# Normalised input turned in 32x32 blocks and carried by transfers; order of weighted inputs, first state and first loads changed

## The reference

```
proj = xn @ in_proj                       # gate z (1024), xBC (1024 + 2N), dt (heads)
xBC  = silu(causal_conv4(xBC) + conv_b)   # 4 taps along time, per channel
dt   = softplus(dt + dt_bias);  A = -exp(A_log)
state_t = state_{t-1} * exp(dt*A) + (dt*x_t) outer B_t      # per head
y_t  = C_t . state_t + D * x_t
A:  out = rmsnorm(y * silu(z)) * norm_w @ out_proj
B:  out = rmsnorm(y) * norm_w * silu(z)  @ out_proj
```

## Time and profile before

| | |
|---|---|
| three runs | 3183.87, 3190.09, 3195.75 us; median 3190.09 |
| the profiled execution | 3185.51 us; its span 3183.8 us |
| mean granted TensorE clock | 0.953 of full |
| mixer A, feed-forward, mixer B, feed-forward | from 0, 1213, 1462 and 2940 us of the span, roughly |
| TensorE, VectorE, ScalarE, GpSimd busy | 89%, 65%, 39%, 31% |

### The profile page before, as it was taken

How to read it: one execution, slowest core, us unless ns; L and a number is a source line. 1 busy time by engine, 2 the same in 40 slices (tenths; PEclk the granted TensorE clock), 3 DMA queues, 4 the chain that set the end, 5 groups by cost and what they waited for, 6 DMA issues and landing times. The chain is left out here.

```text
span 3183.8 us, 54365 instructions
## 1 busy us (share of the span) xinstructions
PE 2839.6 (89%) x19824; PEld 1872.3 (59%) x19824; DVE 2071.5 (65%) x3697; ACT 1248.4 (39%) x2098; POOL 975.0 (31%) x618
## 2 busy tenths in 40 slices
PE   4999999999999996993899999999999999997896
PEld 4666666666666663453666666666666666664453
DVE  3565665665566562485777777877777777776267
ACT  2433434334443331331444444444444444443232
POOL 1232222332233230251233332333233333223135
PEclk9999999999999998996899999999999999998898
DMA  3000000000000005144000000000000000000533
GB/s 117 14 20 26 20 20 20 20 26 26 20 20 20 20 14 225 52 147 158 11 21 20 20 13 20 20 20 10 16 20 20 20 20 13 13 15 29 217 104 134
DMA packets 80673, 140.16 MB, mean 44 GB/s; under 512 B 18120, under 2 KB 18632, under 8 KB 79568
## 3 DMA queue, kind: packets, MB, share of 16 engines
q1 hardware_dynamic: 60048, 126.29, 11.2%
q10 hardware_dynamic: 20544, 12.79, 1.5%
HBM read 104.98 MB, written 33.55 MB: 44 GB/s over the span
## 5 line engine op out<-in xcount | busy, mean ns | idle before, releaser
L525 PE MATMUL work<-b_xnT,b_w_in 128*128 128x256 f32 x2304 | 564.6, 397 | 39.9 <-DVE b_state L1096 29.2
L525 PE MATMUL work<-a_xnT,a_w_in 128*128 128x256 f32 x2176 | 505.0, 388 | 10.0 <-DVE a_w_out L1227 5.8
L525 PEld LDWEIGHTS work<-b_xnT,b_w_in 128*128 128x128 f32 x2304 | 434.5, 195 | 127.8 <-DVE b_state L1096 36.0
L525 PEld LDWEIGHTS work<-a_xnT,a_w_in 128*128 128x128 f32 x2176 | 411.6, 193 | 83.1 <-issue 18.1
L1081 DVE TENSOR_TENSOR b_decay<-b_decay,b_gt 128x1024 f32<-128x1024 f32 x256 | 340.1, 1366 | 27.4 <-ACT b_decay L799 23.4
L799 ACT ACTIVATE b_decay<-seg 128x1024 f32<-128x1024 f32 x256 | 251.6, 1022 | 201.6 <-PE seg L649 200.9
L960 DVE SCALAR_TENSOR_TENSOR b_cv<-b_pre,b_conv_w,b_cv 128x256 f32<-128x256 f32 x480 | 249.6, 548 | 58.8 <-ACT b_cv L745 50.9
L1286 POOL TENSOR_TENSOR a_y<-a_y,a_skip 128x1024 f32<-128x1024 f32 x32 | 106.5, 3327 | 548.2 <-DVE a_y L1070 548.2
L1251 POOL TENSOR_TENSOR rhs<-b_l_side,of_head 128x1024 fp32r<-128x1024 f32 x32 | 83.2, 2600 | 609.3 <-DVE b_l_side L1050 609.3
L630 PE MATMUL work<-a_w_out,a_yz 128*128 128x512 f32 x512 | 248.8, 642 | 21.8 <-ACT a_xnT L729 18.1
L630 PE MATMUL work<-b_w_out,b_yz 128*128 128x512 f32 x512 | 230.8, 604 | 23.7 <-ACT b_xnT L729 15.6
(11 more groups left out here) (309 smaller groups left out, 4733.4 us busy)
## 6 DMA issues: line engine op xcount, KB each, us to landing
f_d_w<-in_L_ffn_d_w SPq DMA_DIRECT2D x4, 4096.0 KB, 24.0
f_x_in<-x_mid ACTq DMA_DIRECT2D x12, 1024.0 KB, 5.9
a_x_in<-in_L_attn_a_x SPq DMA_DIRECT2D x16, 512.0 KB, 3.7
a_x_res<-in_L_attn_a_x SPq DMA_DIRECT2D x32, 256.0 KB, 2.6
x_mid<-a_x_res SPq DMA_DIRECT2D x32, 256.0 KB, 2.0
f_x_res<-x_mid SPq DMA_DIRECT2D x8, 1024.0 KB, 5.5
f_bc_w<-x_mid SPq DMA_DIRECT2D x8, 1024.0 KB, 5.4
b_x_in<-x_mid SPq DMA_DIRECT2D x16, 512.0 KB, 3.6
```

The lines of the kernel that those rows point to most:

```text
L525: mm = nc.tensor.matmul(dst, w_in[:, k, col:col + m], xnT[:, k, :], start=(k == 0), stop=(k == KD - 1))
```

## The change

1. `xn` and the steps "xnT0", "xnT1" with ScalarE's copies are gone. `norm_apply` normalises `x_in` in place; VectorE then turns it in 32x32 blocks (`nc.vector.transpose`) into `turned`, laid out so that each channel block is contiguous. SP carries it to `xnT` in 16 transfers per supertile (`carry`): for each destination group q of 32 partitions and each source group r, 32 partitions with 8 runs of 32 floats. They are issued after "zzb" of the supertile, and "dt" waits for all 16 (256 counts). `carry` stands between `load_x` and the store in SP's `step`.
2. "ident0" moves to the head, between "pout" and "small1". "state0" moves ahead of the last pair of diagonal products, and `state_add(sec, 0)` ahead of the gate.
3. `make_xdt(sec, 0)` moves ahead of "prs" and `make_xdt(sec, 1)` ahead of the first decay product.
4. w_out is multiplied by norm_w inside the first supertile; only "out0" of it waits for `w_out_ready`.
5. For mixer A, x_in, w_in and its small vectors are loaded in the block of the constants. The masks, the feed-forward's vectors and mixer B's vectors are loaded by SP in mixer A's prologue, behind w_out and the next input. In mixer B the gate's part of w_in and w_out are loaded after the first carrying.
6. `lhs` and `rhs` become buffers of each mixer; their sizes stay.

```diff
+def load_in(sp, x_in, w_in, xs_src, w, x_loaded, xbc_loaded):
+    sp.dma_start(x_in[:], xs_src[0]).then_inc(x_loaded, 16)
+    sp.dma_start(w_in[:, :, E:], w["in_proj"].rearrange("(t p) n -> p t n", p=P)[:, :, E:]).then_inc(xbc_loaded, 16)
...
     with nc.Block() as block:
+        @block.sync
+        def _(sp):
+            w = weights[mixers[0].tag]
+            load_in(sp, early["x_in"], early["w_in"], early["xs_src"], w, early["x_loaded"], early["xbc_loaded"])
+            load_z(sp, early["w_in"], w, early["z_loaded"])
         @block.scalar
         def _(act):
...
+                m = mixers[0]
+                load_vectors(act, c["vectors"][m.tag], weights[m.tag], m.H, c["vectors_loaded"][m.tag])
...
-        xn = sb("xn", [P, 2, DM])
+        turned = sb("turned", [P, 4, KD, 2, 32])
         xnT = sb("xnT", [P, KD, SUP])
...
-                    + (["prs"] if prev else []) + ["yoff0a", "yoff0b"] + (["prt"] if prev else [])
-                    + (["xnT0", "xnT1"] if nxt else []) + (["pout"] if prev else []) + ["small1"])
+                    + (["prs"] if prev else []) + ["yoff0a", "yoff0b"] + (["prt", "pout"] if prev else [])
+                    + ["ident0", "small1"])
...
-                if p == 0:
-                    steps += ["ident0"]
+                if p + 1 == NP:
+                    steps += state_steps(0)
                 steps += [f"ydiag0.{2 * p}", f"ydiag0.{2 * p + 1}"]
-            steps += (["z0a"] if nxt else []) + state_steps(0)
+            steps += ["z0a"] if nxt else []
...
+                def carry(n, sec):
+                    if sec:
+                        sp.wait_ge(work_full, sec.full("zzb"))
+                    sp.wait_ge(turned_ready, FREE + 2 * n + 2)
+                    for q in range(4):
+                        for r in range(4):
+                            sp.dma_start(xnT[32 * q:32 * q + 32].rearrange("p k (j r b) -> p r k j b", j=2, r=4)[:, r],
+                                         turned[32 * r:32 * r + 32, q]).then_inc(xnT_loaded, 16)
...
-                def step(i, m, prev, nxt):
+                def step(sec, i, m, prev, nxt):
                     if m is not None:
                         load_x(m)
+                    if nxt is not None:
+                        carry(nxt, sec)
...
+                carry(0, None)
+                if not early:
+                    load_z(sp, w_in, w, z_loaded)
+                sp.dma_start(w_out[:], w["out_proj"].rearrange("(k p) n -> p k n", p=P)).then_inc(out_loaded, 16)
                 load_x(1)
                 load_res(0, 0)
+                if later:
...
-                        pe.wait_ge(xnT_ready, FREE + 2 * n + 2)
+                    if name == "dt":
+                        pe.wait_ge(xnT_loaded, 256 * (n + 1))
...
-                    dve.wait_ge(xnT_ready, FREE + 2 * n)
                     for j in range(2):
-                        nc.vector.tensor_scalar(xn[:, j, :], x_in[:, j, :], mv[:, j, 0:1], ln_r[:, j:j + 1],
+                        nc.vector.tensor_scalar(x_in[:, j, :], x_in[:, j, :], mv[:, j, 0:1], ln_r[:, j:j + 1],
                                                 ALU.subtract, ALU.mult).then_inc(xn_ready, 1)
+                    if not (isinstance(n, int) and n == 0):
+                        dve.wait_ge(xnT_loaded, 256 * n)
+                    for j in range(2):
+                        dve.wait_ge(xn_ready, FREE + 2 * n + j + 1)
+                        nc.vector.transpose(turned[:].rearrange("p q k j b -> p j k q b")[:, j],
+                                            x_in[:, j, :].rearrange("p (k q b) -> p k q b", q=4, b=32)
+                                            ).then_inc(turned_ready, 1)
...
                     masked_gt(sec)
+                    make_xdt(sec, 0)
                     if prev:
                         square_sums(sec, "prs")
                     from_state(sec, 0)
                     if prev:
                         rms_var(sec, "prt")
-                    make_xdt(sec, 0)
+                    make_xdt(sec, 1)
                     slot_mult(sec, 0, 0)
...
-                    make_xdt(sec, 1)
                     if prev:
                         out_add(sec, "pout", i - 1, 1)
+                    else:
+                        norm_into_w_out()
...
                             if g + 1 == NS and NP > 1:
+                                state_add(sec, 0)
                                 gate(sec, 0)
```

More of the change, by code:

```diff
@@ L188, in build_constants, with mixer_phase @@
     return c
-def mixer_phase(nc, sig, before, cfg, c, first_mixer, psum, x_src, x_dst, w):
+def mixer_phase(nc, sig, before, cfg, c, early, later, psum, x_src, x_dst, w):
     H, HP, N, NS = cfg.H, cfg.HP, cfg.N, cfg.slots
@@ L379, in is_use @@
             return not step.startswith(("seg", "ydiag", "ident"))
-        pro_steps = ["xnT0", "xnT1", "dt"] + blocks + ["z0a", "z0b", "z1", "z2", "sums", "small0"]
+        pro_steps = ["dt"] + blocks + ["z0a", "z0b", "z1", "z2", "sums", "small0"]
         epi_steps = ["prs", "prt", "pout"]
@@ L506, in step @@
                         load_res(nxt, 0)
+                carry(0, None)
+                if not early:
+                    load_z(sp, w_in, w, z_loaded)
+                sp.dma_start(w_out[:], w["out_proj"].rearrange("(k p) n -> p k n", p=P)).then_inc(out_loaded, 16)
                 load_x(1)
                 load_res(0, 0)
+                if later:
+                    for b in range(4):
+                        for q in range(4):
+                            sp.dma_start(c["masks"][32 * q:32 * q + 32, b], c["masked_bf"][32 * b:32 * b + 32]
+                                         ).then_inc(c["masks_loaded"], 16)
+                    with nc.allow_non_contiguous_dma(reason="small vectors"):
+                        load_ffn_vectors(sp, c["ffn"], c["ffn_w"], c["ffn_loaded"])
+                        load_vectors(sp, c["vectors"][later.tag], c["weights"][later.tag], later.H,
+                                     c["vectors_loaded"][later.tag])
                 before.clear(sp)
-                step(0, 2, None, 1)
+                step(first(), 0, 2, None, 1)
                 with sp.Fori(0, NSUP - 3) as r:
-                    step(r + 1, r + 3, r, r + 2)
-                step(NSUP - 2, None, NSUP - 3, NSUP - 1)
-                step(NSUP - 1, None, NSUP - 2, None)
+                    step(body(r), r + 1, r + 3, r, r + 2)
+                step(last_but_one(), NSUP - 2, None, NSUP - 3, NSUP - 1)
+                step(last(), NSUP - 1, None, NSUP - 2, None)
                 store(NSUP - 1, 1)
@@ L1128, in out_add, with norm_into_w_out @@
                                                    ).then_inc(out_done, 1)
+                def norm_into_w_out():
+                    dve.wait_ge(out_loaded, 16)
+                    for k in range(KE):
+                        ins = nc.vector.tensor_scalar(w_out[:, k, :], w_out[:, k, :], norm_w[:, k:k + 1], None, ALU.mult)
+                    ins.then_inc(w_out_ready, 1)
                 def supertile(sec, prev, nxt):
@@ L1224, in _ @@
                 exponent_sides(0)
-                dve.wait_ge(out_loaded, 16)
-                for k in range(KE):
-                    ins = nc.vector.tensor_scalar(w_out[:, k, :], w_out[:, k, :], norm_w[:, k:k + 1], None, ALU.mult)
-                ins.then_inc(w_out_ready, 1)
                 supertile(first(), False, True)
```

133 lines of the change are left out of this document (61 added, 72 removed).

## The result

The changed kernel takes 3026.1 us (median of four runs, 3025.1 to 3030.2) against 3189.4 us before it: ratio 0.949, 95% interval 0.947 to 0.951. The profiled execution took 3025.1 us (span 3023.3), before 3185.5 (3183.8). 160.5 us left the span; the forecast was 120.

What follows compares the result with a forecast made beforehand. The prediction took TensorE's issue time, busy 89% of the span, plus its few waits as the bound. 39 + 49 - 8 - 12 + 25 + 14 - 3 + 16 = 120 us off 3185.51 gave 3067 us as median, range 3025 to 3150.

Steps and rivals of the forecast that it cites:

- the low end: Whole kernel: 3025 us, the range's lower bound, taking in issues from 0.38 us and the prologue's bounds.
- The other signs: In the trace: no TensorE transposes; issues of 0.4 to 0.64 us; "dt" waits under 1 us; no wait before "z0b".
- Parts 1 and 3: Heads lose TensorE transposes and waits, gaining 39 and 49 us; 16 carrying transfers make "dt" late, 12 us of new wait.
- The decision point: Before "dt": at 0.93 us per carrying transfer, the wait eats the 132 us that the rest brings.
- Part 2: VectorE in each head: two transposes of 128x512 take 1.4 us for the pair, covered by waiting VectorE has anyway.
- friction per head: VectorE's new order in the heads: 0.3 us charged for each of 28, 8 us.
- Part 1: Heads: transposes, copy waits and waits before "dt" go; 2.8 us in A and 3.5 in B, 14 supertiles each.
- everything hides: Rival, chance 0.17: issues cost 0.38 us, no new wait before "dt" (+12), clock gains up to 15 us; 3040 us.
- Part 4: Before "z0b" in B: the first state's new place removes 29.2 us of waiting, 25 us net; nothing in A.
- Parts 5 and 6: Mixers' starts: scaling w_out in the first supertile gains 14 us less 3; the reordered first loads gain 16 us.
- Part 5: First supertile: scaling w_out there removes waits of 5.78 and 8.01 us, 14 us; 3 us charged for the bare carrying.

Runs made afterwards that it cites:

- carry20: The changed kernel with the last four of a supertile's 16 transfers cut in two, the same bytes in 20 transfers: 162 us slower than the changed kernel.
- old_weighted: The changed kernel with VectorE's weighted inputs (make_xdt) and ident0 back in their old places: 173 us slower than the changed kernel, 10 us slower than before the change.
- old_state: The changed kernel with the first state's matmuls and addition back behind the gate, as before: 40 us slower than the changed kernel.
- hybrid: The changed kernel with inputs 0 and 1 of each mixer turned by TensorE and copied by ScalarE, the other 14 carried: 20 us faster than the changed kernel.
- te_turn: The changed kernel with the input turned by TensorE and copied by ScalarE again, no carrying, all else as changed: 50 us slower than the changed kernel.
- late_pout: The changed kernel with the previous tile's output projection also waiting for ScalarE's first decays in the looped supertiles: 57 us slower than the changed kernel.
- order_alone: The kernel before the change with only the weighted inputs and ident0 in their new order: 53 us faster than the kernel before.

## Why the prediction was near, and where it missed

The median of 3026.1 lies in the range by 1 us, and that is luck: the low end was drawn for issues of 0.38 us, which did not come, and not for the clock, which did. Of the signs that were named, supertiles 2.3 to 2.8 us shorter in A and 4.7 to 5.2 in B hold only for the least periods (2.6 and 5.1), not for the mean (3.9 and 6.3); the first "dt" came at 33.8 us, outside 28 to 33, and the wait of "dt" in the first supertiles was 4.7 and 4.1 us, not 8. The other signs came, but for one wait of 1.05 us before the third "dt" of A.

The working against the span, in us; the forecast's terms are regrouped by stretch (13 heads in the steady part, one in the first supertiles):

```
stretch                                   forecast              measured
A, 13 periods, least period               13 x 2.0 =  26        13 x 2.63 = 34
B, 13 periods, least period               13 x 4.7 =  61        13 x 5.11 = 66
clock steps in them                       0                     17 + 15   = 32
both, start to the third dt               16 + 14 - 3 + 6.7 = 34   7.8 + 18.5 = 26
ends of the mixers, feed-forward          0                     1.5
sum                                       120                   160.5
```

- **Parts 1 and 3, heads and carrying: right in mechanism and size.** 0.611 us an issue, 0.65 with its gap (0.637 forecast), 10.4 us for 16, landing 2.0 us (2.5), start 0.1 us after "zzb" (0.2); "dt" late by 8.0 / 14 = 0.57 us in A and 3.9 / 14 = 0.28 in B (0.5 and 0.3). The masks' issue constant was the right row and their landing was not, as the forecast chose. By the Trainium skill, DMA: Bandwidth & Descriptors, "Bandwidth", whose figures are for loads from HBM that GpSimd issues, the estimate was that the transfers follow each other at about 0.8 us; measured 0.65.
- **The decision point.** The forecast let the carrying cost its lateness and no more, so that 0.93 us a transfer would be break-even. carry20, which is no faster than the kernel before, shows break-even at 2.4 us of added lateness: with 16 transfers that is 0.61 + 2.4 / 15 = 0.77 us each, an estimate. The margin was half of what I thought.
- **Part 2, VectorE: right.** 0.69 us a transpose of 128x512 (0.7 forecast), hidden. By the Trainium skill, VectorE: DVE Perf Modes, "The three transpose paths", whose figure is for bf16, a pair was estimated at 2.5 us; the row says 1.30 for float32. The 0.3 us of friction per head cannot be seen; it is the most likely home of the 0.4 to 0.6 us by which the least periods beat the forecast, though no run isolates it.
- **The order was priced wrongly by itself.** Part 1 takes the 0.47 and 1.36 us before "dt" along, "as the second weighted input is now made before the masks' products", and treats it as a small extra. old_weighted shows that it decides the sign: without it 3199 us. The sum was near only because both edits were made together.
- **The missed term is the clock.** The sum prices stalls by their length and puts the clock at nothing. 32 of the 40 us that are missing are clock steps (36 by the granted clock: 39 us before, 3 after), and before the change 20 of the 21 periods that had one had it right behind these stalls. The numbers were in sight: "z0b" at 3.17 us and 0.97, and the rival *everything hides* had "up to 15 us" for it. That rival came nearest with its time (3040) and was wrong in its reason: the issues did not cost 0.38 us, and the wait it denied is there.
- **Part 4, the state: 25 us forecast.** The stall alone is 1.7 us x 13 = 22; with its clock, 40 by old_state.
- **Parts 5 and 6, the starts: 8 us too high.** The first "dt" of A came 4.0 us earlier, not 7.5: its statistics began at 16.9 us, not 13. ScalarE's last issue of a small vector ended only at 15.2 us (7.87 + 7.28), and the block of the constants could not end before it. B's prologue was 9.5 us shorter (8.8 forecast). The other 5 us are missing between the first and the third "dt", where both mixers together won 12.9 us of 17.7. Part 5 names that the scaling of w_out now stands ahead of the small sums there, but with the bare carrying it charges only 3 us. VectorE's 5.67 us of scaling hold up those sums; in hybrid TensorE waits 4.06 us for them, and in the changed kernel that wait is hidden behind the one for the transfers. TensorE also waits there for GpSimd's y before "ident0", 4.18 us in A and 3.58 in B, a wait the forecast did not have and no run isolates. Still both moves pay: leaving the first loads or the scaling in place costs 19 and 18 us.

Open: which stalls are followed by a step and which are not, and why the first state's place in A changes it. The same 1.36 us in te_turn and 1.95 us in late_pout were followed by one in some supertiles and by none in others; in order_alone B kept its stall of 1.94 us before "z0b" and mostly had none.

## What to carry to other kernels

Price a TensorE stall by its length and by what the clock loses behind it: compare the same group of matmuls behind the stall and elsewhere in the trace, look at the granted clock there, and take the sum. When work leaves one engine, look at what the next engine has queued ahead of the instruction that frees the bank; if it is more than the slack, nothing is won until that queue is reordered. Carrying data by many small transfers is paid per transfer, and pays only where compute covers it; where TensorE is idle anyway, let it do the transposes.

## What the runs showed of the hardware

- Stalls of 1.1 to 2.0 us before a TensorE group were followed, in part of the cases, by 1.7 us more in the matmuls behind, at times 3.0 (8.83 and 10.13 us instead of 7.13 for 16 of 128x512, at a granted clock of 0.81 and 0.70). A stall of 2.97 us was followed by 4.5 us more, at 1.2 instead of 2.4 GHz at first ("dt" 3.60 for 1.96 us, granted clock 0.50). A wait of 0.5 us ("dt" of the changed kernel in A) had a step in 2 of 13 periods.
- An SBUF to SBUF transfer of 32 partitions x 8 runs of 128 B costs SyncE 0.61 us to issue (0.65 with its gap), half the bytes the same, and lands in 2.0 us; behind 6.9 MB of loads 16 issues took 19.3 instead of 10.5 us.
- VectorE's 32x32 block transpose of 128x512 float32 took 0.69 us.
